# Attention products in six banks at the seam to the second layer, with the first two units' vector and TensorE work reordered

## The reference, cut to what matters

```
xn = layernorm(x)
x  = x + attn0(xn) + ffn0(xn)      # attn0: linear attention with 16 heads; ffn0: 2 of 8 experts per token
xn = layernorm(x)
x  = x + attn1(xn) + ffn1(xn)      # attn1: 8 heads in blocks of 64 tokens; ffn1: each expert takes its 512 best tokens
```

## Time and profile before

| | us |
|---|---|
| three runs | 742.98, 743.87, 746.7 (median 743.87) |
| span of the profiled execution, first to last instruction | 743.1 |
| PE busy | 688.5 (93%) |
| DVE busy | 545.0 (73%) |
| ACT busy | 446.2 (60%) |
| POOL busy | 443.7 (60%) |

### The profile page before, as it was taken

The page is one execution under the profiler, slowest core; times in us unless marked ns, Lnnn a source line. Parts: engine busy times, 40 slices in busy tenths (PEclk is TensorE's granted clock), DMA queues, the critical chain, the costliest instruction groups (busy, mean ns, idle before and its releaser), DMA issues.

```text
span 743.1 us, 19839 instructions
## 1 busy us (share of the span) xinstructions
PE 688.5 (93%) x6400; PEld 619.2 (83%) x6400; DVE 545.0 (73%) x1311; ACT 446.2 (60%) x940; POOL 443.7 (60%) x524
## 2 busy tenths in 40 slices
PE   5999998899999899999998999799898899999993
PEld 4898877788999899999977999677677678888883
DVE  5999777766887677878658886699986686666632
ACT  6565476666776677745526888466676664444420
POOL 3577789698997897996422223034354635555363
PEclk9999999999999999999999999899999999999998
DMA  9689752365443434533169985145568755666252
GB/s 255 169 261 290 233 164 65 93 175 133 118 124 113 122 101 135 144 87 113 38 202 302 304 282 171 34 106 127 116 112 205 218 197 136 150 147 163 33 58 28
DMA packets 147015, 111.91 MB, mean 151 GB/s; under 512 B 59361, under 2 KB 137188, under 8 KB 146920
## 3 DMA queue, kind: packets, MB, share of 16 engines
q1 hardware_dynamic: 133720, 84.84, 41.4%
q0 software_dynamic: 12624, 25.35, 13.6%
q10 hardware_dynamic: 576, 0.53, 0.3%
HBM read 66.58 MB, written 40.80 MB: 145 GB/s over the span
## 4 chain that ended last, share of the span: by engine, by line
PE 64%; DVE 8%; issue 5%; ACT 3%; DMA 3%; POOL 2%; SPq 1%; ACTq 1%; POOLq 0%; DVEq 0%
PE banks L987 12%; PE bank L1243 11%; PE bank L951 9%; PE banks L1254 5%; PE bank L1043 5%; PE banks L878 4%; PE bank L962 4%; PE banks L1060 3%; PE bank L934 2%; PE bank L1133 2%; PE bank L1122 1%; PE bank L1150 1%; DVE rw L2031 1%; PE banks L865 1%; PE banks L1219 1%
## 5 line engine op out<-in xcount | busy, mean ns | idle before, releaser
L987 PE MATMUL banks<-r_split,rt_split 128*128 x852 | 111.9, 285 | 4.3 <-ACT rw L1447 1.6
L987 PEld LDWEIGHTS banks<-r_split,rt_split 128*128 128x128 f32 x852 | 105.2, 190 | 6.0 <-issue 5.9
L2385 POOL DMA_INDIRECT ults_by_choice_and_token<-rw,y_id x71 | 80.7, 1137 | 39.8 <-ACT rw L1447 29.1
L1243 PE MATMUL bank<-r_split 128*128 128x512 f32 x384 | 89.6, 391 | 1.3 <-issue 1.1
L951 PE MATMUL bank<-wq_high_or_w_low_split,rt_split 128*128 128x256 f32 x560 | 86.7, 286 | 0.6 <-DVE rt_split L1870 0.6
L2333 POOL DMA_INDIRECT rows_by_expert<-rw,slots x64 | 66.2, 1034 | 32.6 <-issue 16.2
L1243 PEld LDWEIGHTS bank<-r_split 128*128 128x128 f32 x384 | 71.4, 188 | 16.3 <-issue 1.9
L2487 POOL DMA_INDIRECT out_x<-r,idx x32 | 50.2, 1568 | 52.9 <-DVE r L2222 45.2
L951 PEld LDWEIGHTS bank<-wq_high_or_w_low_split,rt_split 128*128 128x128 f32 x560 | 76.0, 189 | 1.1 <-DVE rt_split L1870 1.1
L1895 DVE TENSOR_TENSOR rt_split<-rw,rt_split 128x512 fp32r<-128x512 f32 x71 | 65.2, 949 | 11.4 <-ACT rt_split L1440 11.0
L1870 DVE TENSOR_TENSOR rt_split<-r,rt_split 128x512 fp32r<-128x512 f32 x56 | 49.1, 916 | 17.5 <-ACT rt_split L1369 17.5
(11 more groups left out here) (300 smaller groups left out, 1864.7 us busy)
## 6 DMA issues: line engine op xcount, KB each, us to landing
rt<-in_w SPq DMA_DIRECT2D x24, 512.0 KB, 4.8
rw<-rows_by_expert SPq DMA_DIRECT2D x71, 128.0 KB
r<-in_w SPq DMA_DIRECT2D x16, 512.0 KB, 8.8
rt<-ults_by_choice_and_token SPq DMA_DIRECT2D x32, 256.0 KB, 4.1
rw<-in_x SPq DMA_DIRECT2D x16, 256.0 KB
rw<-x_layer SPq DMA_DIRECT2D x16, 256.0 KB
x_plus_bias<-rw SPq DMA_DIRECT2D x16, 256.0 KB, 3.3
rows_layer<-rt SPq DMA_DIRECT2D x16, 256.0 KB, 2.8
```

The lines of the kernel that those rows point to most:

```text
L987: last = pe.matmul(bank[6 + t % 2][:, 0:D], hidden_T(h, t, c), w[:, ds(e2, 1), o + c * D:o + (c + 1) * D], start=n == 0, stop=n == 3 * HC - 1)
L1243: last = pe.matmul(bank[2 * (hb % 2) + k][:, :], w[:, o:o + P], x[:, s.par, c, :], start=n == 0, stop=n == 3 * DC - 1)
L2385: pool.indirect_dma_start(y0_d[:, :], bass.IndirectOffsetOnAxis(y_id[:, t:t + 1].bitcast(I32), 0), c_y[:, t % XB, :], None, bounds_check=l ...
```

## The change

The seam's products get six banks instead of two (4, 5, 6, 7, 3, 2 in turn), so that the product of tile i waits for the sum of tile i-6; the third of them waits for the last expert result to be out of its bank, a wait that stood before the bias product till now. The bias product moves from bank 7 to bank 1.

On PE, unit 0's transposes move behind the last product (from behind tile 29's). Then comes a wait until the sums of tiles up to 27 are done (they free banks 2 and 3), queries and keys of unit 0, a wait for the bias, the transposes of unit 1, and values and scores of unit 0. Before, unit 1's transposes stood ahead of all of unit 0's projections.

On DVE, `combine(0, 0)`, `combine(0, 1)` and moments 0 stand together behind tile 24's sum, scale 0 behind 25's, `combine(1, 0)` behind 27's, then `low_xT(0)`, `combine(1, 1)` and moments 1 behind 28's, scale 1 behind 29's. The sums of tiles 30 and 31 come last, then unit 2.

ACT, POOL and SP keep their orders.

```diff
--- before.py
+++ after.py
@@ -355,6 +355,15 @@
         def group(t):
             return t // 2 if t < T1 else t - ND
 
+        LATE_BANKS = (4, 5, 6, 7, 3, 2)
+        AS = len(LATE_BANKS)
+
+        def ao_place(i):
+
+            if i < NE:
+                return bank[4 + i % 2][:, 0:D]
+            return bank[LATE_BANKS[(i - NE) % AS]][:, 0:D]
+
         def x_tile(i):
             if i < NE:
                 return q_x[:, i % 4, :, :]
@@ -872,10 +881,14 @@
                 pe.wait_ge(qrot, i + 1)
                 if i == 0:
                     pe.wait_ge(m_sb, NB)
-                if i >= 2:
+                if 2 <= i < NE:
                     pe.wait_ge(ao_sb, i - 1)
+                elif i >= NE:
+                    pe.wait_ge(ao_sb, max(NE, i - AS + 1))
+                if i == NE + 2:
+                    pe.wait_ge(y_sb, ST0)
                 for r in range(DC):
-                    last = pe.matmul(bank[4 + i % 2][:, 0:D], xT_all[:, r, i * P:(i + 1) * P], m_all[:, i // BT, r, :],
+                    last = pe.matmul(ao_place(i), xT_all[:, r, i * P:(i + 1) * P], m_all[:, i // BT, r, :],
                                      start=r == 0, stop=r == DC - 1)
                 last.then_inc(ao_ps, 1)
 
@@ -1015,9 +1028,8 @@
             def bias_of_values():
 
                 pe.wait_ge(wq1_r, 3)
-                pe.wait_ge(y_sb, ST0)
                 for c in range(DC):
-                    last = pe.matmul(bank[7][:, 0:D], bv1_b[:, c, :], wo1_s[:, c, :], start=c == 0, stop=c == DC - 1)
+                    last = pe.matmul(bank[1][:, 0:D], bv1_b[:, c, :], wo1_s[:, c, :], start=c == 0, stop=c == DC - 1)
                 last.then_inc(bo1_ps, 1)
 
             def transpose_unit(v):
@@ -1070,9 +1082,13 @@
                 attend(i)
                 if i == NE:
                     bias_of_values()
-                elif i == NT - 3:
-                    transpose_unit(Unit(0, 0, 2))
-            for u in (1, 2, 3):
+            transpose_unit(Unit(0, 0, 2))
+            pe.wait_ge(ao_sb, NE + 2 * AS)
+            queries_keys(Unit(0, 0, 2))
+            pe.wait_ge(bo1_ps, 2)
+            transpose_unit(Unit(0, 1, 2))
+            values_scores(Unit(0, 0, 2))
+            for u in (2, 3):
                 transpose_unit(Unit(u // 2, u % 2, 2))
                 project_before(Unit(u // 2, u % 2, 2))
             with pe.Fori(2, NU // 2) as m:
@@ -1899,7 +1915,7 @@
             def add_attention(i):
                 dve.wait_ge(ao_ps, i + 1)
                 dve.wait_ge(xq_r, i + 1)
-                dve.tensor_tensor(x_tile(i), bank[4 + i % 2][:, 0:D].rearrange("p (c n) -> p c n", c=DC), x_tile(i),
+                dve.tensor_tensor(x_tile(i), ao_place(i).rearrange("p (c n) -> p c n", c=DC), x_tile(i),
                                   ALU.add).then_inc(ao_sb, 1)
 
             dve.drain().then_inc(table_r, 1)
@@ -1982,16 +1998,22 @@
                 add_attention(i)
                 if i == NE + 1:
                     dve.wait_ge(bo1_ps, 1)
-                    dve.tensor_tensor(bo1_s[:, :], bo1_s[:, :], bank[7][:, 0:D], ALU.add).then_inc(bo1_ps, 1)
-                elif i in (NE + 8, NE + 9):
-                    combine(0, i - NE - 8)
-                elif i in (NE + 10, NE + 13):
-                    moments_unit((i - NE) // 13)
-                elif i in (NE + 11, NE + 14):
-                    scale_unit((i - NE) // 14)
-                if i in (NE + 11, NE + 12):
-                    combine(1, i - NE - 11)
-            for u in range(NU + 1):
+                    dve.tensor_tensor(bo1_s[:, :], bo1_s[:, :], bank[1][:, 0:D], ALU.add).then_inc(bo1_ps, 1)
+                elif i == NE + 8:
+                    combine(0, 0)
+                    combine(0, 1)
+                    moments_unit(0)
+                elif i == NE + 9:
+                    scale_unit(0)
+                elif i == NE + 11:
+                    combine(1, 0)
+                elif i == NE + 12:
+                    low_xT(0)
+                    combine(1, 1)
+                    moments_unit(1)
+                elif i == NE + 13:
+                    scale_unit(1)
+            for u in range(2, NU + 1):
                 if 2 <= u < NU:
                     combine(u, 0)
                     combine(u, 1)
```

## The result

The kernel after takes 748.18 us (median of 20 runs, 745.39 to 751.48). The kernel before, run beside it, takes 745.02 (20 runs, 742.79 to 749.79); the 743.87 that the prediction started from was the median of three. The ratio is 1.0036, with a 95% interval from 1.0020 to 1.0051: some 2.7 us slower, too little to call a change by the half per cent that was set as the bound. The predicted 745.8 was 743.87 plus 1.9; the ratio on the same 743.87 gives 746.5, inside the predicted range of 742.6 to 747.8, and the raw median of 748.18 lies 0.4 above that range.

A forecast was written before the change was run, and what follows sets the result against it. PE sets the seam's pace until about 385, then a chain over DVE, SP, DMA, DVE and ACT. Late load 1.4 plus clock fall 0.5 is 1.9 slower: 743.87 becomes 745.8 us, range 742.6 to 747.8.

The forecast's parts named there:

- The main step: At the seam, products run without gaps, but DVE's later last sum delays SP's stores and unit 3's load: 1.4 us later.
- The 1.4 of the order: DVE's new order makes unit 0's first store, then unit 3's load and combine, 1.4 us later through SP's queue.
- The wait for the last expert result and the bias product in bank 1: Wait moved to the third product, near 377.8, costs nothing; bias product keeps its place and length.
- the clock's 0.5: Behind PE's 3.0 gap, the clock falls in unit 1's projections; 0.8, 0.2 or 0 us, taken as 0.5.
- PE's time to spare: Between unit 1's projections and unit 2's queries, PE has 0.9 us of slack to absorb a clock fall.
- Unit 2's holder: Unit 2's scaled rows wait for the buffer that unit 0's store must leave, 399.2, taken as 399.3; by DVE 398.8.
- the price of PE's order: Unit 0 projected ahead of unit 1's transposes: the 2.4 us gained become a 3.0 gap ahead of unit 2's transposes.
- gaps won: Rival: the three removed waits for a bank, 1.76 us together, are won, giving 742.1; chance 0.10.
- the load not held back: Rival: SP's queue gives the 1.4 back and unit 3 starts when DVE is free, -0.3, 743.6; chance 0.12.
- the long fall of the clock: Rival: 6.0 us at half clock on unit 1's projections and the next, total 3.5 us slower, 747.4; chance 0.13.
- all idle time gone: Rival: all 5.2 us of PE's idle time before unit 2's queries goes, giving 738.7; chance 0.02.

The follow-up runs named there:

- vector_order: Kernel before with the six banks and DVE's new order, PE's order as before; ratio to the kernel before 1.0011 (0.9992 to 1.0029).
- sums_first: Kernel after with the sums of tiles 28 to 31 made in one piece ahead of unit 0's low part; ratio to the kernel before 0.9994.
- filler_to_end: Kernel after with 30 unread matmuls in PE's gap, the last 10 waiting until unit 0's rows left the buffer; ratio to the kernel before 1.0042.
- pool_later: Kernel after with POOL's sum for unit 2 waiting for DVE's scale; one execution, tile 16's product to unit 2's queries 32.5 us, no ratio.
- pe_order: Kernel after with DVE's order of the kernel before, so six banks and PE's new order; ratio to the kernel before 1.0030.
- banks_alone: Kernel before with only the six banks and their waits, PE's and DVE's orders unchanged; ratio to the kernel before 1.0002.
- load_ahead: Kernel after with SP issuing unit 3's loads of expert results ahead of tile 28's store; ratio to the kernel before 1.0017.
- load_ahead_full: Kernel after with unit 3's loads issued ahead of tile 28's store and 30 unread matmuls in PE's gap; ratio to the kernel before 1.0029.
- filler: Kernel after with 24 unread matmuls put into PE's gap ahead of unit 2's transposes; ratio to the kernel before 1.0035.

## Why the prediction was right, and where it was off

The main step held. The products need no gap, but behind them DVE and SP set the end, and DVE's new order holds SP's queue. The prediction's times (in brackets) count with a start 0.40 earlier: the last product ends at 390.27 (389.9), DVE is free for the low part 0.57 early (0.75), unit 0's first store starts at 396.04 (395.7), unit 3's combine at 401.47 (401.0) and the gap ahead of unit 2's transposes is 3.24 (3.0). The 1.4 of the order is 1.45 in the trace; vector_order makes 1.33 of it alone, and sums_first takes it away.

The wait for the last expert result and the bias product in bank 1 cost nothing; the products run through both.

**The mis-sized term** is the clock's 0.5. It measured 1.08 (1.07 by filler_to_end). The loss itself was right: 4.61 less 2.83 is 1.78, where I had 1.7. I had taken a middle between a fall that begins inside the gap (0.2) and one in the projections alone (0.8); it was the second. The rest is PE's time to spare, 0.7 (1.78 less 1.08) instead of 0.9; POOL's hold of the scale, a term that the prediction lacks, took some 0.3 of it, by pool_later.

**Unit 2's holder** was named wrongly, which cost that 0.3: the prediction had the buffer until 399.3 (399.7 with the start moved), and it was DVE's scale beside POOL until 399.87; in pool_later, without that, the buffer holds it, 24.02 behind the start of the stretch (predicted 24.1), and 0.30 is gained. And the price of PE's order was taken as a gap moved on; pe_order shows that it also holds ACT when the low part is late, a term that the kernel after avoids since its low part is early.

The rivals: gaps won, no (banks_alone); the load not held back, no (401.47); the long fall of the clock, no (3.4 at half speed, as in the sum, and below the 6.4 from which it decides); all idle time gone, no. The 5.2 of that rival was the stretch less a sum of work; PE's own busy time left only 3.24 to win before, and leaves 5.34 now. Of the 2.7 by the ratio, the stretch gives 2.53. The 1.57 behind it in the profiled execution goes with another fall, in the attention stage: there the clock was still 0.50 from 483 to 487.9, a stretch of the kernel after, where before it had come back (0.98 in the same stretch).

```profile
483.00:487.90 4.90, 4.90 (x60) 3.74 (x60) 4.57 (x16) 1.50 (x3) 0.00 (x0) 0.50 0.36 55
```

That isn't where the 2.7 comes from. From 60 to 95 us behind unit 2's queries the mean granted clock is 0.85 in all twelve other kernels, also in those no slower than before (banks_alone, sums_first, tail_late), and 0.90 in the one profile of the kernel before; from unit 2's queries to the end it takes 337.7, the others 338.3 to 340.7.

## What to carry to other kernels

Before giving a busy engine more buffers, look who ends the waits behind the place: here 1.76 of gaps went away and PE waited one step later, because DVE and a queue of stores set the end. When work is moved on one engine, count what stands behind it in every in-order queue, SP's and ACT's too; four sums of 0.33 moved behind a low part cost 2.5 by way of a store queue, a load, a POOL sum beside DVE's scale, and a clock that fell behind the gap. Where two paths are late side by side, taking away one (load_ahead) may show nothing until the other is shorter as well. And matmuls that fill a gap are not free of other effects: measure what the DMAs do beside them.

## What the runs showed of the hardware that was not expected

**POOL holds a DVE instruction.** The 128x2 scale with both inputs in SBUF took 1.16 in after, 1.21 in vector_order and 1.17 in load_ahead, each time ending with a POOL sum of 1.26 to 1.29 that had begun 0.1 before it. Before, where POOL's sum had begun 1.04 earlier, it took 0.26 and ended with it. At 394.29 in after it takes 0.16, and in pool_later too, where POOL came behind it. In load_ahead_full a 128x256 piece of a combine that began inside POOL's sum took 1.04 instead of 0.47. Sums with one input in PSUM took their usual 0.4 beside POOL. The Trainium skill (SBUF — State Buffer, "Who interferes with whom") says that a VectorE instruction with two SBUF inputs contends with a GpSimd one that reads SBUF, and that the lock is exclusive; the trace agrees, with 1.16 for 0.16.

**The clock and the length of a gap.** It fell behind gaps of 3.24 (after, load_ahead), 2.94, 3.28 and 3.53, and once behind 1.55 (filler, where matmuls had run until the gap); it didn't behind 1.58 (sums_first), 1.60 and 1.99 (banks_alone), 1.07 or 0.75. The gap's length alone doesn't decide; what does stays open.

**The issue of a load varies.** Unit 3's two loads of expert results took 1.05 to issue in after and 2.52 in filler_to_end, with the same order on SP and only PE's matmuls added; such pairs further down the queue took 1.0 to 2.8 in all kernels. The cause is open.
